# Turning the normalised tokens of groups 1 to 7 in 32x32 squares on VectorE, from pieces reloaded out of DRAM, in an attention and mixture-of-experts kernel

## The chip, the cores and the metric

One core of a Trainium2 chip runs the whole kernel. The metric is the device time of one execution in microseconds, as the median over several runs. A core has TensorE (matmul, with a separate weight load), VectorE, ScalarE, GpSimd, and SyncE (SP), which here only issues DMAs. Each engine runs its own instructions in order and waits for others on semaphores.

## What is computed

The input is 4 x 1024 tokens of 512 features. Each token is layer-normalised; attention and experts read the result xn, and both are added to x.

```python
xn = (x - mean) / sqrt(var + eps)
q, k, v = silu(xn @ Wq), silu(xn @ Wk), silu(xn @ Wv)      # 16 heads of 32
o = lightning_attn(q, k, v, log_decay)                     # chunks of 128 tokens, decaying state
o = group_rmsnorm(o * sigmoid(xn @ Wg1 @ Wg2)) * norm_w
y = x + o @ Wo
y = y + experts(xn)       # softmax(xn @ Wg), top 2 of 8; relu(xn @ w1) @ w2, capacity 1280
```

All of it is in float32. Products run as three passes of parts: each operand is split into a high part (rounded to the type that TensorE takes at full rate) and a low part (the rest), and high x high, high x low and low x high are summed.

## The kernel before

The 4096 tokens are 32 tiles of 128. Four tiles make a group (`g`, 0 to 7; `TPG` = 4, `SUPERS` = 8). Each group has 4 units (`i`, 0 to 3; `u = 4 g + i`), one for 4 heads. TensorE's loop over the units, in program order: `score`, `update_states` (a unit ahead where `updated_ahead` says so), `project_gate`, the k and the q projection of the next unit, `turn_kd`, `attend`. In unit 1 of a group the four output projections of the group before follow, and in unit 3 the small projection (gate and logits, `project_small`), `turn_logits`, and the four v projections of the next group.

For the projections the tokens must lie with features on partitions: xnT. A tile `xn[:, j, :]` (`j = t % 4`) is made by `normalise` on VectorE and stored to the DRAM tensor `xn_rows` by SP (`store_xn`), since the experts gather tokens from there. In unit 2 of a group TensorE turns the next group's four tiles with `turn_xn`: 4 transposes of 128x128 a tile, into four PSUM banks. ScalarE rounds them to `xnT_hi` (`xnT_high`), VectorE subtracts to `xnT_lo` (`xnT_low`); the k projection of the next group's first unit stands in unit 3. The second v projection of the next group waits for `g1_lo_made`, the low parts of the gate's inner product, made by VectorE (`gate_low`), behind ScalarE's `gate_high`, which is itself behind ScalarE's `oT_high` of unit 1.

VectorE's order in a unit: `states`, `mask` (4 instructions), `mean_square`, `scale_heads`, `turn_back` (of two units before), in unit 2 the four `xnT_low`, `gate_output`, `turn_gated`, `oT_low`. In unit 1 four `add_residual` follow, one for each output projection, with `norm_pair` between them and two `normalise` behind them; in unit 3 `choose`, `norm_pair` and two `normalise`. GpSimd multiplies kT and qT by their decays (`decayed_k`, `decayed_q`), raises small tensors to the power -1/2 (`head_scales`, `norm_scale`) and issues indirect DMAs for the routing.

SP's queue is one order written out by hand. At the start: four x tiles, Wq, Wk (eight pieces of 256 KB), the small weights, wg2, norm_w, four stores of xn, Wv and Wo. After that, in unit 1: four `store_y`, two `store_xn`, two `load_x`, then four `load_residual`. Each DMA stands behind its wait, and everything behind it waits too.

The weights `wq`, `wk`, `wv` are loaded as rows 128 t to 128 t + 127, since the k order of a projection is that of the turned tokens. The experts' weights are already loaded in another k order (rows q, t, d), because gathered tokens are turned in 32x32 squares by VectorE (`turn_gathered`).

## Time and profile before

| | us |
|---|---|
| median of 3 runs | 1984.32 |
| lowest, highest | 1983.89, 1984.41 |
| profiled execution | 1986.43 |
| its span on the core | 1984.7 |
| first group's start to its unit 0 | 0 to 32 |
| attention, units 0 to 31 | 32 to 532 |
| experts | 532 to the end |

The granted clock of TensorE is 1.0 in every stretch. All times in the rows below are microseconds from the span's start, in one profiled execution. A duration in a timeline overlaps with that of the next matmul, because they are pipelined; the pitch is the distance of two starts. "idle before" is how long the engine had nothing to do, with the instruction that released it.

### The profile page before, as it was taken

The numbers are of one execution on the slowest core, as the hardware profiler recorded it, in microseconds if no ns is written. First come the engines' busy times: TensorE is split into PE (matmuls) and PEld (weight loads), VectorE is DVE, ScalarE is ACT, GpSimd is POOL, SyncE is SP. The second block draws the span as 40 slices with busy tenths as digits, with TensorE's granted clock in tenths as the row PEclk, the third lists the DMA queues.
The fourth block names the chain that finished last, engine by engine and source line by source line (L and its number), as shares of the span: only waits on it lengthen the run. The fifth ranks groups of instructions, "written<-read, shape, count | busy, mean of one in ns | idle before, by whom it ended". The sixth has DMA issues, their size and how long they took to land.

```text
span 1984.7 us, 28995 instructions
## 1 busy us (share of the span) xinstructions
PE 1972.2 (99%) x11672; PEld 1631.0 (82%) x11672; DVE 906.7 (46%) x1839; ACT 552.5 (28%) x994; POOL 730.1 (37%) x608
## 2 busy tenths in 40 slices
PE   9999999999999999999999999999999999999998
PEld 7888888888888888888888888888888888888887
DVE  8777676777753234224323422432343234334311
ACT  6322232223332123124212312321242123123211
POOL 4645454545343324313342431333143324233321
PEclk9999999999999999999999999999999999999999
DMA  6112122211452134315233421522162125224121
GB/s 206 67 66 87 43 68 68 84 63 48 131 153 39 47 75 125 42 55 126 66 67 74 126 42 56 125 65 42 47 159 45 43 51 157 37 62 102 42 33 22
DMA packets 85638, 151.50 MB, mean 76 GB/s; under 512 B 18432, under 2 KB 18432, under 8 KB 85488
## 3 DMA queue, kind: packets, MB, share of 16 engines
q1 hardware_dynamic: 61312, 105.64, 16.8%
q0 software_dynamic: 24176, 43.76, 13.0%
q8 instruction: 106, 1.74, 0.4%
q14 instruction: 44, 0.36, 0.1%
HBM read 109.82 MB, written 39.53 MB: 75 GB/s over the span
## 4 chain that ended last, share of the span: by engine, by line
PE 97%; DVE 1%; SPq 1%; DMA 0%; issue 0%; POOL 0%; ACT 0%; DVEq 0%
PE bank L1383 47%; PE bank L1687 35%; PE bank L1519 5%; PE bank L1437 2%; PE bank L1508 2%; PE bank L1390 1%; PE bank L1502 1%; PE bank L1743 1%; PE bank L1730 1%; PE bank L1472 1%; PE bank L1411 1%; PE bank L1482 1%; DMA attn_raw<-in_L_attn_Wv 0%; PE bank L1531 0%; SPq L446 0%
## 5 line engine op out<-in xcount | busy, mean ns | idle before, releaser
L1303 DVE SCALAR_TENSOR_TENSOR h_lo<-bank,h_hi 128x512 fp32r<-128x512 f32 x254 | 175.3, 690 | 722.9 <-ACT h_hi L904 683.7
L682 POOL DMA_INDIRECT gathered<-xn_rows,gather_row x304 | 315.5, 1038 | 483.6 <-DVE x_blocks L1153 316.8
L1383 PE MATMUL bank<-xT_lo,w_hi 128*128 128x512 f32 x1024 | 398.5, 389 | 0.5 <-issue 0.5
L1383 PE MATMUL bank<-xT_hi,w_hi 128*128 128x512 f32 x1024 | 398.7, 389 | 0.0
L1383 PE MATMUL bank<-xT_hi,w_lo 128*128 128x512 f32 x1024 | 398.4, 389 | 0.0
L1687 PE MATMUL bank<-w_hi,h_hi 128*128 128x512 f32 x1016 | 395.2, 389 | 0.0
L1687 PE MATMUL bank<-w_lo,h_hi 128*128 128x512 f32 x1016 | 395.2, 389 | 0.0
L1687 PE MATMUL bank<-w_hi,h_lo 128*128 128x512 f32 x1016 | 395.2, 389 | 0.0
L904 ACT ACTIVATE h_hi<-bank 128x512 fp32r<-128x512 f32 x254 | 151.7, 597 | 795.5 <-PE bank L1383 756.3
L703 POOL DMA_INDIRECT out_rows<-y,add_row x64 | 103.9, 1624 | 435.7 <-ACT y L897 419.6
L1383 PEld LDWEIGHTS bank<-xT_lo,w_hi 128*128 128x128 f32 x1024 | 192.2, 188 | 40.9 <-issue 1.0
L1383 PEld LDWEIGHTS bank<-xT_hi,w_hi 128*128 128x128 f32 x1024 | 192.2, 188 | 40.8 <-issue 0.7
L1383 PEld LDWEIGHTS bank<-xT_hi,w_lo 128*128 128x128 f32 x1024 | 192.2, 188 | 39.9
L1687 PEld LDWEIGHTS bank<-w_lo,h_hi 128*128 128x128 f32 x1016 | 190.7, 188 | 39.8
L1687 PEld LDWEIGHTS bank<-w_hi,h_lo 128*128 128x128 f32 x1016 | 190.7, 188 | 39.6
L1687 PEld LDWEIGHTS bank<-w_hi,h_hi 128*128 128x128 f32 x1016 | 190.7, 188 | 39.4
L1123 DVE TENSOR_TENSOR w_lo<-raw_weights,w_hi 128x512 fp32r<-128x512 f32 x256 | 167.8, 684 | 84.8 <-ACT w_hi L802 64.9
L802 ACT CAST w_hi<-raw_weights 128x512 fp32r<-128x512 f32 x256 | 150.0, 618 | 98.3 <-DMA raw_weights<-in_L_ffn_w 78.8
L636 POOL TENSOR_TENSOR head_scale<-mean_sq,minus_half 128x16 f32<-128x16 f32 x32 | 104.4, 3264 | 20.7 <-DVE mean_sq L1025 20.2
L628 POOL DMA_INDIRECT slot_table<-record,slot_no x64 | 65.5, 1024 | 103.7 <-DVE slot_no L1069 47.4
L1018 DVE TENSOR_TENSOR scores<-bank,intra_decay 128x512 f32<-128x512 f32 x128 | 79.2, 681 | 0.4 <-PE bank L1437 0.3
L1163 DVE TENSOR_TENSOR xT_lo<-x_blocks,xT_hi 128x512 fp32r<-128x512 f32 x68 | 48.4, 711 | 52.3 <-ACT xT_hi L845 52.3
(225 smaller groups left out, 2298.5 us busy)
## 6 DMA issues: line engine op xcount, KB each, us to landing
raw_weights<-in_L_ffn_w SPq DMA_DIRECT2D x256, 256.0 KB
x_in<-in_L_attn_x SPq DMA_DIRECT2D x32, 256.0 KB, 4.0
xn_rows<-xn SPq DMA_DIRECT2D x32, 256.0 KB
x_res<-in_L_attn_x SPq DMA_DIRECT2D x32, 256.0 KB, 4.9
out_rows<-y_attn SPq DMA_DIRECT2D x28, 256.0 KB
gathered<-xn_rows,gather_row POOLq DMA_INDIRECT x304
out_rows<-y,add_row POOLq DMA_INDIRECT x88, 5.8
attn_raw<-in_L_attn_Wq SPq DMA_DIRECT2D x4, 256.0 KB, 4.7
```

The source lines that it names most:

```text
L628: pool.indirect_dma_start(table[:, :], bass.IndirectOffsetOnAxis(ap=slot_no[:, t, i:i + 1], axis=0), record[:, t, i, :], None, bounds_chec ...
L636: g_.tensor_tensor(head_scale[:, u % 2, :], mean_sq[:, u % 2, :], minus_half[:, :], ALU.pow).then_inc(S["head_scale_ready"], 1)
L682: pool.indirect_dma_start(xg[:, nth % 2, q * P:(q + 1) * P], None, xn_pieces, bass.IndirectOffsetOnAxis(ap=gather_row[:, col, q:q + 1], ax ...
L703: pool.indirect_dma_start(out[:, :], bass.IndirectOffsetOnAxis(ap=add_row[:, col:col + 1], axis=0), y[:, i, :], None, compute_op=ALU.add). ...
L802: a.copy(unit_parts(u)[0], raw[:, u % UNITS, :]).then_inc(S["ffn_hi"], 1)
L904: a.activation(h_parts(e, j, f)[0][:, 0:n * P], h_bank[f % 2][:, 0:n * P], ACT.Relu).then_inc(S["h_hi_ready"], 1)
L1018: v_.tensor_tensor(by_chunk(scores[:, r, :]), by_chunk(sc[r][:, :]), decay_cols(intra_decay[:, u % GROUPS * HPG + r, :]), ALU.mult).then_i ...
L1123: v_.tensor_tensor(lo, raw[:, u % UNITS, :], hi.bitcast(F32), ALU.subtract).then_inc(S["ffn_lo"], 1)
L1303: v_.scalar_tensor_tensor(lo[:, 0:n * P], h_bank[f % 2][:, 0:n * P], 0.0, hi[:, 0:n * P].bitcast(F32), ALU.max, ALU.subtract).then_inc(S[" ...
L1383: last = mm(dest, at(left[l], t), at_r(right[r], t), start=(i == 0), stop=(i == n - 1))
L1519: last = mm(bank[:, :], oT[l][:, t, part], (w_hi["o"], w_lo["o"])[r][:, t, :], start=(start and t == ks[0] and l == r == 0), stop=(stop an ...
L1687: last = mm(y_bank[i][:, :], hx[:, part], wx[c][:, f % FPC, :], start=(f == 0 and l == 0), stop=(f == FT - 1 and l == 2))
```

## The change

VectorE's transpose works on 32x32 squares: it turns each square in place, and doesn't move squares between partitions. So the tile must come with its feature quarters on the four partition quadrants. For groups 1 to 7 SP now reloads each tile from `xn_rows` after it was stored: four DMAs, one for each 32 tokens, put feature quarter q on quadrant q. VectorE turns the tile with one instruction, tile j into the space of tile j - 1 (tile 0 into a new buffer). The k order is then (q, t, d), and the weights of q, k, v, gate and router are loaded in the same order by `by_quad`. The first group is still turned by TensorE, but into the same order, with 16 small matmuls a tile (`turn_by_quads`).

```diff
+        def xn_blocks(j):
+            return xn_first_blocks[:, :] if j == 0 else xn[:, j - 1, :]
...
+        def by_quad(w):
+            return w.rearrange("(q t d) n -> t q d n", q=QUADS, t=DT)
...
+            def reload_pieces(t):
+                j = t % TPG
+                sp.wait_ge(xn_stored[j], 16 * (t // TPG + 1))
+                for i in range(QUADS):
+                    first = t * P + i * HD
+                    sp.dma_start(xn[:, j, i * P:(i + 1) * P], xn_dram[first:first + HD, :].rearrange("s (q f) -> q s f", q=QUADS)
+                                 ).then_inc(xn_pieces_loaded[j], 16)
...
-            sp.dma_start(small_raw[:, :, 0:HD], wg1.rearrange("(t p) n -> p t n", p=P)).then_inc(S["small_loaded"], 16)
-            sp.dma_start(small_raw[:, :, HD:], w_route.rearrange("(t p) n -> p t n", p=P)).then_inc(S["small_loaded"], 16)
+            for t in range(DT):
+                sp.dma_start(small_raw[:, t, 0:HD], by_quad(wg1)[t]).then_inc(S["small_loaded"], 16)
+                sp.dma_start(small_raw[:, t, HD:], by_quad(w_route)[t]).then_inc(S["small_loaded"], 16)
...
+            def turn_pieces(t):
+                j = t % TPG
+                dve.wait_ge(xn_pieces_loaded[j], 16 * QUADS * (t // TPG))
+                wait(dve, ("xn_turned", t))
+                v_.transpose(xn_blocks(j), xn[:, j, :]).then_inc(S["xn_turned"], 1)
...
+            def turn_by_quads(bank, rows_of_tile):
+                for t in range(DT):
+                    for q in range(QUADS):
+                        rows, first = slice(q * HD, (q + 1) * HD), q * P + t * HD
+                        last = mm(bank[rows, t * P:(t + 1) * P], rows_of_tile[:, first:first + HD], ident[:, :], start=True, stop=True)
+                return last
...
+            def project_next_k(g):
+                pe.wait_ge(S["xnT_hi_made"], TPG * (g + 1))
+                for nth, (w_part, x_part, t) in enumerate(hi_hi + lo_hi + hi_lo):
+                    if nth == 2 * DT:
+                        pe.wait_ge(S["xnT_lo_made"], TPG * (g + 1))
+                    last = mm(proj[1][:, :], w_part["k"][:, t, 0:P], x_part[:, t, :], start=(nth == 0), stop=(nth == 3 * DT - 1))
+                last.then_inc(S["k_projected"], 1)
...
-                if i == 2 and g < SUPERS - 1:
-                    pe.wait_ge(S["masked"], HPG * (u + 1))
-                    turn_xn(g + 1, lambda j: pe.wait_ge(S["k_ready" if j == 2 else "q_ready"], u + 2) if j > 1 else None)
```

The waits on `xnT_lo_made` in `score` and ahead of the gate projection of unit 3 are gone; the k projection in unit 3 (`project_next_k`) begins with the passes that need high parts only. On ScalarE `xnT_high` waits for the q projection as well, and `copy_kd` moves between its second and third tile.

TensorE at the hand-over from group 1 to group 2, unit 2 into unit 3 of group 1. Before:

```order
L1383 MATMUL bank<-xnT_lo,wq_hi 128x512
L1383 MATMUL bank<-xnT_hi,wq_lo 128x512
L1390 MATMUL bank<-ident,xn 128x128 x16
L1390 MATMUL bank<-ident,kdT 128x128 x3
L1502 MATMUL bank<-qdT,carry 128x128
L1502 MATMUL bank<-qdT,state 128x128 x3
L1508 MATMUL bank<-scores,v 32x128 x16
L1437 MATMUL bank<-qT,kT 128x128 x16
L1482 MATMUL bank<-v,kd 32x32 x12
L1472 MATMUL bank<-g1T_parts,wg_parts 128x512
L1383 MATMUL bank<-xnT_hi,wk_hi 128x512
```

And now:

```order
L1430 MATMUL bank<-xnT_hi,wq_lo 128x512
L1437 MATMUL bank<-ident,kdT 128x128 x3
L1554 MATMUL bank<-qdT,carry 128x128
L1554 MATMUL bank<-qdT,state 128x128 x3
L1560 MATMUL bank<-scores,v 32x128 x16
L1489 MATMUL bank<-qT,kT 128x128 x16
L1534 MATMUL bank<-v,kd 32x32 x12
L1524 MATMUL bank<-g1T_parts,wg_parts 128x512
L1613 MATMUL bank<-xnT_hi,wk_hi 128x512 x4
L1613 MATMUL bank<-xnT_hi,wk_lo 128x512 x4
L1613 MATMUL bank<-xnT_lo,wk_hi 128x512 x4
```

The 16 transposes of xn are gone, and the four passes with the low parts of the tokens stand last in the k projection.

VectorE in the same hand-over, from the end of unit 1 (`gated` is the gated attention output, `normed` the normalised one). Before:

```order
L1098 STREAM_TRANSPOSE turned_odd<-gated 128x512
L1118 TENSOR_TENSOR y_attn<-bank,x_res 128x512
L976 BN_STATS stats<-x_in 128x6 x2
L978 BN_AGGR moments<-stats 128x2
L979 BN_AGGR moments<-stats 128x2
L980 TENSOR_SCALAR var_eps<-moments 128x2
L1118 TENSOR_TENSOR y_attn<-bank,x_res 128x512 x3
L986 TENSOR_SCALAR xn<-x_in,moments,rstd 128x512 x2
...
L1108 STREAM_TRANSPOSE normed<-squares 128x512
L993 TENSOR_TENSOR xnT_lo<-bank,xnT_hi 128x4x128 x4
L1094 SCALAR_TENSOR_TENSOR gated<-tanh_g,bank 128x512
```

And now:

```order
L1140 STREAM_TRANSPOSE turned_odd<-gated 128x512
L1035 STREAM_TRANSPOSE xn_first_blocks<-xn 128x512
L1035 STREAM_TRANSPOSE xn<-xn 128x512
L1160 TENSOR_TENSOR y_attn<-bank,x_res 128x512
...
L1160 TENSOR_TENSOR y_attn<-bank,x_res 128x512
L1021 TENSOR_SCALAR xn<-x_in,moments,rstd 128x512 x2
L1160 TENSOR_TENSOR y_attn<-bank,x_res 128x512 x2
...
L1150 STREAM_TRANSPOSE normed<-squares 128x512
L1035 STREAM_TRANSPOSE xn<-xn 128x512 x2
L1027 TENSOR_TENSOR xnT_lo<-xn_first_blocks,xnT_hi 128x4x128
L1027 TENSOR_TENSOR xnT_lo<-xn,xnT_hi 128x4x128 x3
```

Two transposes stand ahead of the first residual and two ahead of the low parts; the two normalisations have moved ahead of the last two residuals; and the low parts read the turned tile from SBUF, where they read a PSUM bank.

SP's queue in unit 1 of the same group (`y_attn` is a finished tile of attention output). Before:

```order
L434 DMA out_rows<-y_attn 128x512 x4
L426 DMA xn_rows<-xn 128x512 x2
L422 DMA x_in<-in_L_attn_x 128x512 x2
L430 DMA x_res<-in_L_attn_x 128x512 x4
L426 DMA xn_rows<-xn 128x512 x2
```

And now:

```order
L454 DMA out_rows<-y_attn 128x512 x2
L437 DMA xn_rows<-xn 128x512 x2
L454 DMA out_rows<-y_attn 128x512
L445 DMA xn<-xn_rows 128x1x128 x8
L454 DMA out_rows<-y_attn 128x512
L433 DMA x_in<-in_L_attn_x 128x512 x2
L450 DMA x_res<-in_L_attn_x 128x512 x4
```

The two stores of xn have moved ahead of the last two of y, and eight reloads stand between, the last four of them for tile 3.

## Rows read from the trace of the kernel before

**Rows 1.** The page's part 4, shares of the chain that ended last, by engine.

```profile
PE 97%; DVE 1%; SPq 1%; DMA 0%; issue 0%; POOL 0%; ACT 0%; DVEq 0%
```

**Rows 2.** TensorE's waits, whole span: us in total, times, longest us.

```profile
PE bank L1508 <- DVE scores L1018: 1.0, 1, 1.0
```

**Rows 3.** The chain in order of time, group 1: start us, us, what.

```profile
103.78 0.33 PE bank L1390 x3
...
106.20 11.11 PE bank L1519 x48
...
124.31 2.07 PE bank L1390 x19
```

**Rows 4.** Timeline of TensorE, group 1: start us, us, engine, line, instruction.

```profile
124.15 1.91 PE L1390 MATMUL bank<-ident,xn 128*128 128x128 f32 x16
...
129.99 0.40 PE L1383 MATMUL bank<-xnT_hi,wk_hi 128*128 128x512 f32 x1
...
142.95 0.39 PE L1383 MATMUL bank<-wv_hi,xnT_hi 128*128 128x512 f32 x1
```

**Rows 5.** Timeline of ScalarE, units 2 and 3 of group 1.

```profile
124.84 2.05 ACT L757 CAST xnT_hi<-bank 128x512 fp32r<-128x512 f32 x4
...
138.57 0.62 ACT L808 CAST oT_hi<-normed 128x512 fp32r<-128x512 f32 x1
```

**Rows 6.** Timeline of VectorE, units 1 to 3 of group 1.

```profile
109.19 0.69 DVE L1118 TENSOR_TENSOR y_attn<-bank,x_res 128x512 f32<-128x512 f32 x1 [1.68 <-PE bank L1519]
...
117.96 0.99 DVE L986 TENSOR_SCALAR xn<-x_in,moments,rstd 128x512 f32<-128x512 f32 x2
...
123.60 0.17 DVE L1025 TENSOR_SCALAR mean_sq<-sum_sq 128x16 f32<-128x16 f32 x1
...
125.46 2.48 DVE L993 TENSOR_TENSOR xnT_lo<-bank,xnT_hi 128x512 fp32r<-128x512 f32 x4 [0.35 <-ACT xnT_hi L757]
128.36 0.69 DVE L1094 SCALAR_TENSOR_TENSOR gated<-tanh_g,bank 128x512 f32<-128x512 f32 x1 [0.42 <-PE bank L1508]
...
135.82 0.71 DVE L1108 STREAM_TRANSPOSE normed<-squares 128x512 f32<-128x512 f32 x1
139.23 0.69 DVE L1112 TENSOR_TENSOR oT_lo<-normed,oT_hi 128x512 fp32r<-128x512 f32 x1 [2.70 <-ACT oT_hi L808]
...
140.98 0.69 DVE L1012 CAST g1T_parts<-bank 32x512 fp32r<-32x512 f32 x1
```

**Rows 7.** Timeline of GpSimd, units 2 and 3 of group 1.

```profile
123.85 3.31 POOL L636 TENSOR_TENSOR head_scale<-mean_sq,minus_half 128x16 f32<-128x16 f32 x1 [0.52 <-DVE mean_sq L1025]
128.50 1.28 POOL L589 TENSOR_TENSOR qdT<-qT,q_decay 128x512 f32<-128x512 f32 x1 [1.33 <-PE bank L1508]
...
133.61 1.29 POOL L582 TENSOR_TENSOR kdT<-kT,k_decay 128x512 f32<-128x512 f32 x1 [1.05 <-ACT kT L777]
```

**Rows 8.** Timelines of GpSimd, then VectorE, unit 0 of group 0.

```profile
37.86 1.29 POOL L582 TENSOR_TENSOR kdT<-kT,k_decay 128x512 f32<-128x512 f32 x1
...
37.89 1.43 DVE L1083 SCALAR_TENSOR_TENSOR state<-state,chunk_decay,update 128x128 f32<-128x128 f32 x1
39.35 0.35 DVE L1084 SCALAR_TENSOR_TENSOR carry<-state,chunk_decay,update 128x128 f32<-128x128 f32 x1
```

**Rows 9.** SP's timeline; then DMA issues: KB each, median us to landing.

```profile
6.94 0.47 SPq L453 DMA_DIRECT2D small_raw<-in_L_attn_Wg  x1
...
x_in<-in_L_attn_x SPq DMA_DIRECT2D x32, 256.0 KB, 4.0
...
small_raw<-in_L_attn_Wg SPq DMA_DIRECT2D x1, 64.0 KB, 5.9
```

**Rows 10.** Timeline of TensorE: first group's start, and gathered tiles at 519.

```profile
9.06 2.02 PE L1390 MATMUL bank<-ident,xn 128*128 128x128 f32 x16
...
12.24 1.16 PE L1550 MATMUL bank<-xnT_hi,wq_hi 128*128 128x512 f32 x4 [0.29 <-ACT xnT_hi L757]
...
518.85 2.83 PE L1531 MATMUL bank<-ident,y 128*32 128x128 f32 x96
```

More of the change, by code:

```diff
@@ L255, in build @@
         x_res_loaded = [sem(f"x_res_loaded{i}") for i in range(TPG)]
+        xn_pieces_loaded = [sem(f"xn_pieces_loaded{i}") for i in range(TPG)]
         xn_stored = [sem(f"xn_stored{i}") for i in range(TPG)]
@@ L474, in _ @@
                         store_xn(t)
+                    for t in range(TPG, 2 * TPG):
+                        reload_pieces(t)
                     for t in range(2 * TPG, 3 * TPG):
@@ L487, in _ @@
                 if i == 1 and g > 0:
-                    for j in range(TPG):
-                        store_y(TPG * (g - 1) + j)
+                    store_y(TPG * (g - 1))
+                    store_y(TPG * (g - 1) + 1)
                     if g < SUPERS - 1:
@@ L755, in xnT_high @@
                 act.wait_ge(S["xn_turned"], t + 1)
-                wait(act, ("k_projected", GROUPS * (t // TPG)))
-                a.copy(xnT_hi[:, :, j * P:(j + 1) * P], turned_xn(t)).then_inc(S["xnT_hi_made"], 1)
+                wait(act, ("k_projected", GROUPS * (t // TPG)), ("q_projected", GROUPS * (t // TPG)))
+                a.copy(token_cols(xnT_hi, j), turned_xn(t)).then_inc(S["xnT_hi_made"], 1)
             def weights_high(n, ts=range(DT)):
@@ L864, in _ @@
                     for j in range(TPG):
+                        if j == 2:
+                            copy_kd(u + 1)
                         xnT_high(TPG * (g + 1) + j)
-                if i == GROUPS - 1 and g < SUPERS - 1:
-                    copy_logits(g + 1)
-                if u < ATTN_UNITS - 1:
+                elif u < ATTN_UNITS - 1:
+                    if i == GROUPS - 1:
+                        copy_logits(g + 1)
                     copy_kd(u + 1)
@@ L1242, in _ @@
                     oT_low(u - 2)
+                if i == 1 and g < SUPERS - 1:
+                    turn_pieces(TPG * (g + 1))
+                    turn_pieces(TPG * (g + 1) + 1)
                 if i == 1 and g > 0:
@@ L1527, in turn_first @@
                 pe.wait_ge(S["masked"], HPG * (ATTN_UNITS - 1) + sc.index(first_bank[i]) + 1)
-                for t in range(DT):
-                    for q in range(QUADS):
-                        rows, first = slice(q * HD, (q + 1) * HD), q * P + t * HD
-                        last = mm(first_bank[i][rows, t * P:(t + 1) * P], y[:, i, first:first + HD], ident[:, :], start=True, stop=True)
-                last.then_inc(S["x_turned"], 1)
+                turn_by_quads(first_bank[i], y[:, i, :]).then_inc(S["x_turned"], 1)
             pe.wait_ge(S["consts_made"], 6)
@@ L1540, in _ @@
             keep_clock(40)
-            turn_xn(0)
+            turn_first_xn()
             keep_clock(8)
```

56 lines of the change are left out of this document (34 added, 22 removed).

## The prediction

> **What bounds the kernel now.** I read the chain of work that ended last first: 97% of the span lies on TensorE, and VectorE, ScalarE, GpSimd and the queues together have a few per cent [rows 1]. Then TensorE's own waits: once it is set up, the longest is 1.0 us, once, for masked scores [rows 2]. So the kernel is a single line of TensorE work, and an instruction taken from it gives back its whole pitch, as long as the engine that takes over its job is not late. The question is therefore asked at the places where TensorE will newly have to wait. The stretch that matters is the hand-over from one group of 512 tokens to the next, seven times in the first 450 us; the experts behind it are not touched.
>
> **1. The transposes that go.** In group 1 the chain shows 3 transposes of kdT in 0.33 us, and 19 transposes (16 of xn and 3 of kdT) in 2.07 us [rows 3]. The 16 of xn therefore cost 2.07 - 0.33 = 1.74 us, 0.109 each. (Their duration in the timeline, 1.91 us together, overlaps with what follows [rows 4].) Seven hand-overs lose them: 7 x 1.74 = 12.2 us. TensorE has nothing to put in their place, since the order shows 112 of them gone and no new matmul in the loop.
>
> **2. The first group.** It keeps its transposes on TensorE but turns by quads: 64 small matmuls of 32 weight columns in place of 16. The same form in before, three tiles for the experts, took 2.83 us [rows 10], so 0.94 a tile against 2.02 / 4 = 0.50. The first tile can start at 9.06; the last ends at 12.8 in place of 11.1, and the first projection, which already waited 0.29 for the high parts of the last tile [rows 10], starts about 1.4 later. Besides this, SP issues the small weights in 8 DMAs in place of 2: 6 x 0.47 = 2.8 us [rows 9] by which wg2, norm_w, the stores of xn and Wv are issued later. What the landing does with it is not clear: small_raw took 5.9 us from issue to landing against 4.0 for an x tile four times its size [rows 9], so these DMAs wait in a line for the 3 MB ahead of them, and a later issue shortens that wait. The two delays run side by side, not one after the other. Whether there is slack is seen at the end of this start: TensorE waited 1.0 us for the scores of unit 0 [rows 2], so VectorE's chain is the late one there and hands every delay on. Bounds 1.4 (the turning alone) and 2.8 (the issue alone); I take **1.8**, nearer the first, since the queue looked full.
>
> **3. The pieces come back in time, by little.** VectorE normalises tiles 2 and 3 of the next group after the second out-projection now. Four out-projections take 11.11, 2.78 each [rows 3], the first residual starts at 109.19 [rows 6], so the second ends near 112.6 and the two tiles are written at 113.1 and 113.6. A store has no landing time in the trace; an x tile of the same size takes 4.0 [rows 9], so tile 2 is stored at 117.2, 4 reloads take 4 x 0.47 = 1.9 on SP, 4 more end at 121.0, and the last lands 4.0 later at 125.0. VectorE reaches its two transposes near 124.8 (its mean of squares ends at 123.77 [rows 6], two 0.7 us operations follow, all up to 0.9 us earlier since the two normalisations of 117.96 [rows 6] have moved ahead). Nothing is lost, or 0.2. Queued behind SP's wait for the store: the fourth y store, two x tiles and four residual tiles, none needed for 40 us. A page speaks against such a round trip: the Trainium skill, "DMA: Bandwidth & Descriptors", section "Anatomy of one DMA", gives each DMA about 2 us of fixed cost, most of it the receipt, longest when DRAM is written. Worked out from its figures (an estimate) the store would take 2.6 and the last reload 2.2, earlier than my 4.0 each; by that the term would be nothing.
>
> **4. High parts.** ScalarE starts them at 124.84 as before and does four in 2.05 [rows 5]; copy_kd now stands between (0.4), so they end near 127.4. TensorE comes to them 1.74 earlier than before: 129.99 - 1.75 = 128.24 [rows 4]. 0.8 us of slack. It needs the low parts only after eight matmuls, at 130.0, since the order of its passes has changed.
>
> **5. VectorE's added work and its lock.** Two transposes of 0.71 [rows 6] stand in unit 1 ahead of the first residual, where VectorE was idle for 1.68 us [rows 6]: nothing. Two more (1.3 by their pitch) stand in unit 2 ahead of the low parts. VectorE's line from there runs without a rest to 136.53 (start 135.82 plus 0.71 [rows 6]); it then waited 2.70 us for ScalarE's oT_hi, which itself waits for TensorE [rows 5, 6]. New end of that line: 136.53 + 1.3 - 0.9 (normalisations gone) - 0.77 (its waits of 0.35 and 0.42 around 125.46, for things that now come earlier) = 136.2. TensorE's side allows oT_hi from 138.57 - 1.75 = 136.8. By this alone nothing is late.
>
> But xnT_low now reads both operands from SBUF; so far one came from PSUM. The trace shows what such an instruction meets: a state update of two SBUF operands, otherwise 0.35 us, took 1.43 while GpSimd's kdT product ran from 37.86 for 1.29 [rows 8]. GpSimd's product qdT waits for the attention and started at 128.50; its pow from 123.85 ended at 127.16, now up to 0.9 earlier [rows 7]. So qdT now starts at 128.50 - 1.75 = 126.75, into the third and fourth low part: about 1.2 late. That pushes the state updates behind the start of the next kdT, 133.61 - 1.75 = 131.86 [rows 7], and they lose 1.3 more. With both, VectorE's line ends at 138.7, oT_hi starts there, and g1T_parts is complete 3.1 later as before (138.57 to 141.67 [rows 5, 6]), at 141.8. TensorE wants it for the second v projection at 142.95 - 1.75 = 141.2 [rows 4]: **0.6 late**. With one block or none it is in time. If the two small waits don't go, 1.35. Bounds 0 and 1.35 for each of six hand-overs; I take 0.6, since the arithmetic puts both products on top of VectorE: 6 x 0.6 = 3.6. The first hand-over is worse: unit 1 of group 0 has no out-projection, so no gap for its two transposes, and no normalisation is taken off. That is 2.2 more on VectorE's line, half of which I let pass through: 1.7 (0.2 to 2.6).
>
> The page's rule: the Trainium skill, "SBUF — State Buffer", section "Who interferes with whom", says that a VectorE instruction with two SBUF inputs and a GpSimd one that reads SBUF exclude each other for the whole instruction, whichever came first. The trace agrees in the row of 1.43. It doesn't say who wins when VectorE's next instruction is already queued; if VectorE, this term is nothing.
>
> **Sum**: -12.2 + 1.8 + 3.6 + 1.7 = -5.1 us. The profiled span was 1984.7, so 1979.6; the median of the runs is 1984.3, hence **1979.2**.
>
> **The rivals.**
> *A clean gain.* VectorE keeps the lock through its four low parts, or GpSimd's products fall between; then the hand-overs cost 0.2 in all and the start 1.4: -10.6, **1973.7**. For it: VectorE's rest of 2.70 us and the 1.2 us (142.95 - 141.7) that TensorE had in hand. Against it: both products move earlier by just what TensorE gains.
> *VectorE eats the gain.* Both blocks in each hand-over and the small waits stay: 6 x 1.35 = 8.1, first one 2.6, start 2.0: +0.5, **1984.8**. For it: VectorE has 2 x 1.3 us more per group, and whatever it is late by, TensorE gets no faster.
> *The round trip is late, and it gets slower.* If a store and a reload each take 5.9 us, as small_raw did [rows 9], and all 8 issues lie between: stored 119.1, issued 122.9, landed 128.8, and the high part of tile 3 is ready 1.4 later, 130.2 against 128.24: 2.0 per hand-over, 7 x 2.0 + 1.8 + 3.6 - 12.2 = +7.2, **1991.5**. It decides from a landing after about 127.8, 1.5 per hand-over. Against it: SP's queue is empty at 113, with 3 MB ahead of it only at the start.
> That the change would not do what it says has no case: the order has the transposes gone.
>
> **How the numbers follow.** Forecast 0.42, with its own range of 1976 to 1981.5; clean gain 0.26; gain eaten 0.25; slower 0.07. The range 1973.5 to 1986.0 takes in the first three and leaves out most of the last and a little on the fast side. What a measurement of this kernel can tell from no change is 0.2%, 4.0 us: faster means under 1980.3. The clean gain and some four fifths of the forecast lie there, 0.60; the rest of the forecast and the eaten gain make 0.33 for the same; slower 0.07.
>
> **What would show it.** The chain should have 16 transposes fewer in each hand-over, 1.74 us between the q projection and kdT's transposes gone. Step 2: the first projection at about 13.6, unit 0's attention at about 44. Step 3: no wait of the transposes on the reloads. Step 5: one or two of the low parts, and a state update, drawn out to about 1.3 us with a GpSimd product beside them, and TensorE idle before the second v projection on g1T_parts. If TensorE waits for xnT_hi in place of that, step 3 or 4 is wrong; if it waits for nothing, step 5.

## The result, and the profile after

The changed kernel takes 2017.9 us (median of 6 runs, 2016.0 to 2019.3) where the kernel before takes 1984.2 on the same chip (6 runs, 1983.5 to 1984.8). The ratio is 1.017, with a 95% interval of 1.0157 to 1.0184: 1.7% slower. Forecast were 1979.2, a range of 1973.5 to 1986.0, and a chance of 0.07 for slower. The profiled execution spans 2015.6 us, 30.9 more than before.

TensorE's waits are the first view to compare with [rows 2], where 1.0 us for scores was the longest once the engine was set up. Columns as there: engine, place, what it waited for, us in total, times, longest.

```profile
PE bank L1430 <- DVE wv_lo L1046: 10.4, 4, 4.8
PE bank L1598 <- ACT xnT_hi L789: 6.3, 1, 6.3
PE bank L1430 <- DVE g1T_parts L1054: 4.2, 7, 0.9
PE bank L1598 <- ACT wk_hi L799: 4.1, 2, 2.2
PE bank L1586 <- POOL ident L578: 2.7, 1, 2.7
PE bank L1430 <- issue: 2.3, 1, 2.3
PE bank L1613 <- DVE xnT_lo L1027: 0.7, 1, 0.7
PE bank L1560 <- DVE scores L1060: 0.3, 1, 0.3
```

Three rows wait for weights or for what stands behind them (wv_lo, wk_hi, and xnT_hi, whose copies stand behind Wq's on ScalarE). All of their seven waits lie in the first 53 us. The row of g1T_parts is the wait that the prediction's step 5 named; it comes once in each hand-over. The 2.3 for "issue" comes up below.

ScalarE's timeline at the start shows what the weights wait for (start us, us, line, instruction, and in brackets the idle time ahead of it with its releaser):

```profile
9.56 0.63 ACT L799 ACTIVATE wq_hi<-attn_raw 128x512 fp32r<-128x512 f32 x1 [2.42 <-DMA attn_raw<-in_L_attn_Wq]
12.23 0.63 ACT L799 ACTIVATE wq_hi<-attn_raw 128x512 fp32r<-128x512 f32 x1 [2.04 <-DMA attn_raw<-in_L_attn_Wq]
14.89 0.63 ACT L799 ACTIVATE wq_hi<-attn_raw 128x512 fp32r<-128x512 f32 x1 [2.03 <-DMA attn_raw<-in_L_attn_Wq]
17.58 0.63 ACT L799 ACTIVATE wq_hi<-attn_raw 128x512 fp32r<-128x512 f32 x1 [2.06 <-DMA attn_raw<-in_L_attn_Wq]
18.12 2.03 ACT L789 CAST xnT_hi<-bank 128x512 fp32r<-128x512 f32 x4
```

One piece of 256 KB arrives every 2.67 us; in before, four copies of wq_hi began and ended within 2.67 us. Now the same stretch by windows, first after, then before (stretch and its length; PE, PEld, DVE, ACT and POOL busy; granted clock, DMA share of 16 engines, GB/s):

```profile
12.00:15.00 3.00, 2.04 (x48) 1.60 (x36) 0.00 (x0) 0.74 (x2) 0.13 (x1) 1.00 0.26 98
...
12.00:34.00 22.00, 11.62 (x69) 8.23 (x58) 5.56 (x9) 6.35 (x11) 0.13 (x1) 0.70 0.30 97
```

```profile
4.00:10.00 6.00, 6.00 (x45) 5.89 (x43) 5.43 (x17) 4.90 (x13) 2.69 (x7) 1.00 1.05 396
```

After moves 98 GB/s with a share of 0.26, before 396 with 1.05: four engines' worth of work against sixteen, at the same rate for each busy engine (98 / 0.26 and 396 / 1.05 are both 377). The load of a weight tile now reads four strips of 32 rows, with the strip as its outermost dimension, of size 4. The Trainium skill, "DMA: Bandwidth & Descriptors", section "Why a DMA increments its semaphore by 16 and not by 1", says that the number of engines is the largest one up to 16 that divides the sizes of the slowest dimension on both sides; by that, 4. The trace agrees: a share of 0.26 is close to 4 of 16, 0.25.

The granted clock is the second thing in that stretch: 0.70 over 12 to 34 us, and 0.50 over 45 to 55, where 0.50 is the lower of the two levels (1.2 in place of 2.4 GHz). TensorE had idled 6.25 us, 1.95, 2.17 and 4.76 before it. In before the clock was 1.00 in both stretches.

SyncE's queue, which issues the loads (start us, us taken by the issues):

```profile
3.13 2.44 SPq L467 DMA_DIRECT2D attn_raw<-in_L_attn_Wq  x4
5.61 11.02 SPq L467 DMA_DIRECT2D attn_raw<-in_L_attn_Wk  x4
16.67 2.55 SPq L475 DMA_DIRECT2D small_raw<-in_L_attn_Wg  x1
...
34.18 3.29 SPq L467 DMA_DIRECT2D attn_raw<-in_L_attn_Wv  x4
```

Issuing Wk took 11.02 us; in before it took 1.87. So the queue doesn't only deliver late, it also takes new work late, and Wv, issued at 12.84 before, goes out at 34.18.

With the start of each unit's score products as milestones (from TensorE's timelines, us) the whole span can be laid side by side. "Hand-over" is the unit that ends a group, unit 3 to 4, 7 to 8 and so on; the transposes stood in the unit before it.

| stretch | before | after | difference |
|---|---|---|---|
| start to the first score | 32.29 | 65.57 | +33.3 |
| unit 0 | 10.87 | 9.54 | -1.3 |
| units 2, 6, ... 26 | 11.29, 10.98, 10.87, ... | 9.55, 9.24, 9.13, ... | 7 x -1.74 = -12.2 |
| first hand-over | 22.85 | 25.93 | +3.1 |
| six others | 22.84 to 23.11 | 23.79 to 24.40 | +6.9 |
| unit 29 | 23.13 | 20.86 | -2.3 |
| from unit 31 to the end of the span | 1469.2 | 1472.6 | +3.4 |

That makes 30.9. The expected gain is in the table to the hundredth, 1.74 for each of seven groups. Ahead of it stand 33 us at the start, for which the prediction has 1.8.

The row of unit 29 is not the change's, since kernels of the changed kind have the 2.3 us too. TensorE has two short stops for "issue" there (0.34 and 0.46 us in before) in the profiles of before and of experiments 1 to 8, which take 23.1 to 23.3 us for the unit, and none in those of the changed kernel and of experiments 9 to 12, which take 20.9. The profiled execution of before took 1986.4 us, 1.6 more than the slowest of its six other runs. So the two profiles lie 30.9 us apart where the medians lie 33.7 apart.

### The profile page after: what moved, and what is told of

Read it like the earlier page. It is cut to its first block, busy times and chain, and to the rows that moved or that the text cites. A ratio compares the mean times of both kernels' runs of the same rounds, so it can differ in the third digit from the quotient of the medians.

```text
span 2015.6 us, 29141 instructions
## 1 busy us (share of the span) xinstructions
PE 1977.5 (98%) x11672; PEld 1624.9 (81%) x11672; DVE 939.2 (47%) x1867; ACT 554.9 (28%) x994; POOL 736.2 (37%) x608
## 4 chain that ended last, share of the span: by engine, by line
PE 88%; DVE 6%; SPq 2%; issue 2%; DMA 1%; ACT 1%; POOL 0%; DVEq 0%
PE bank L1430 43%; PE bank L1743 35%; PE bank L1571 4%; DVE scores L1060 1%; PE bank L1799 1%; PE bank L1786 1%; PE bank L1489 1%; PE bank L1560 1%; DVE xnT_lo L1027 1%; DMA attn_raw<-in_L_attn_Wv 1%; PE bank L1554 1%; SPq L467 1%; PE bank L1437 1%; DMA xn<-xn_rows 1%; DVE xn L1035 0%
## 5 line engine op out<-in xcount | busy, mean ns | idle before, releaser
L1743 PEld LDWEIGHTS bank<-w_hi,h_lo 128*128 128x128 f32 x1016 | 190.7, 188 | 39.6
```

The lines of the kernel that those rows point to most:

```text
L1743: last = mm(y_bank[i][:, :], hx[:, part], wx[c][:, f % FPC, :], start=(f == 0 and l == 0), stop=(f == FT - 1 and l == 2))
```

## The experiments

Twelve kernels in three sets, each set on one chip with its own runs of before. The medians of before were 1987.3, 1986.8 and 1984.6; the differences below are to these. My theory was that the loads' pattern is the slow start; the rivals were the order in SyncE's queue, the turning by quads with the clock, and at the hand-overs VectorE held up by GpSimd (the lock of step 5) against the order of its copies and ScalarE's.

### 1. Plain weight loads in the changed kernel

```
-                rows = w[u % DT * P:(u % DT + 1) * P, :] if u // DT == WSET.index("o") else by_quad(w)[u % DT]
-                sp.dma_start(attn_raw[:, u % UNITS, :], rows).then_inc(attn_raw_loaded[u % UNITS], 16)
+                sp.dma_start(attn_raw[:, u % UNITS, :], w[u % DT * P:(u % DT + 1) * P, :]).then_inc(attn_raw_loaded[u % UNITS], 16)
```

> The changed kernel with one edit: the twelve loads of Wq, Wk and Wv take plain blocks of 128 rows again (the sums over features then pair wrong rows, so the attention's values are wrong; the work is the same; Wg1 and the router keep their order, so the routing is unchanged). Theory 1, the loads' pattern: each 256 KB load in four strips of 32 rows kept only a quarter of the DMA engines busy (98 to 105 GB/s and a share of 0.26 where before showed about 400 GB/s), and TensorE was 33 us late at the first score; the loads take about 0.65 us again, the first score comes within 3 us of the 32.3 us of before, and the time is 1979 to 1984 us, faster than before by up to 5. Theory 2, the queue's order (six more small loads and sixteen reloads on SyncE's queue): the start stays more than 15 us late, time over 2000. Theory 3, turning by quads on TensorE and the lower clock behind it: the start stays late, time over 2000.

Measured: 1992.4 us, 5.0 above before (ratio 1.003, 1.0018 to 1.0041) where the change cost 33.7. I had expected a time below that of before. The first score is at 37.8: 27.8 of the 33.3 us are back. Of what is left, SyncE's timeline shows the part of the small loads: one of the eight issues takes 2.19 us, and Wv goes out at 18.00 in place of 12.84, TensorE waiting 2.0 for it:

```profile
9.67 2.19 SPq L474 DMA_DIRECT2D small_raw<-in_L_attn_Wg  x1
...
18.00 2.63 SPq L466 DMA_DIRECT2D attn_raw<-in_L_attn_Wv  x4
```

So the pattern is the bulk, and the queue's order is real too: a part of the second theory. The hand-overs take as long as in the changed kernel (25.91 us the first, 23.80 to 24.40 the others); experiments 4 to 6 take that up.

### 2. The pattern alone, in the kernel before

```
-                sp.dma_start(attn_raw[:, u % UNITS, :], w[u % DT * P:(u % DT + 1) * P, :]).then_inc(attn_raw_loaded[u % UNITS], 16)
+                rows = w[u % DT * P:(u % DT + 1) * P, :] if u // DT == WSET.index("o") else w.rearrange("(q t d) n -> t q d n", q=QUADS, t=DT)[u % DT]
+                sp.dma_start(attn_raw[:, u % UNITS, :], rows).then_inc(attn_raw_loaded[u % UNITS], 16)
```

> The kernel before with one edit: its twelve loads of Wq, Wk and Wv take four strips of 32 rows each (the attention's values are then wrong, the work is the same). Theory 1, the pattern alone: 30 to 34 us slower than before, 2014 to 2018 us, with weight loads of about 2.66 us each at about 100 GB/s and a granted clock below 1.0 in the first 100 us. Theories 2 and 3 (the queue's order, the first group's turning): 1984 to 1986 us.

Measured: 2014.7 us, 27.4 above before (1.0137, 1.012 to 1.0154), the first score at 62.1, a clock of 0.56 over 12 to 34 us. That is less than the 30 to 34 expected; the eight small loads and the turning by quads aren't there, and the first score comes 3.5 us ahead of the changed kernel's. With nothing else of the change in it, the pattern alone costs 27 us.

### 3. The same order of features from another pattern

```
+                q, first = u % DT, u // DT * DT % UNITS
+                sp.dma_start(attn_raw[q * HD:(q + 1) * HD, first:first + DT, :],
+                             w[q * P:(q + 1) * P, :].rearrange("(t d) n -> d t n", t=DT)).then_inc(attn_raw_loaded[u % UNITS], 16)
```

> The changed kernel, whole and with the same order of features in Wq, Wk and Wv, but each of the same twelve loads of 256 KB brings another share: the 32 partitions of one quad for all four tiles of a matrix, with 32 rows as its outer dimension, where the changed kernel's load brings all 128 partitions of one tile with four strips as its outer dimension. A matrix is then whole only with its fourth load. Theory 1 in the form 'as many DMA engines as the outer dimension gives': the engines' share is near 1.0, a load takes 0.7 us, the start is 1 to 3 us behind that of plain blocks, time 1980 to 1987 us. Theory 1 in another form, 'rows that don't lie in one block in memory are slow' or 'few partitions are slow': loads stay at 100 to 200 GB/s, time over 1995. Theories 2 and 3: time over 2000.

Measured: 2000.9 us, 13.5 above before (1.007, 1.0054 to 1.0087). Neither form of theory 1 alone: the share is full, the rate is not. Its window:

```profile
12.00:15.00 3.00, 2.49 (x64) 2.05 (x52) 0.69 (x1) 2.63 (x6) 0.13 (x1) 1.00 1.08 209
```

All 16 engines are busy (1.08) and move 209 GB/s, half of before's 396 at 1.05. With an outer dimension of 32 the engines are all at work again, as they should be by the rule of the Trainium skill cited above. Something else in this form then halves what each engine moves. Rows are of 2 KB in all three forms; what differs from the plain block is that a load fills 32 partitions and not 128, and that each partition takes four rows that lie 32 rows apart in DRAM. Which of these it is I didn't separate.

### 4. Natural order everywhere

The order of features is turned round: the normalising instruction writes permuted columns, and after the 32x32 turning each tile of 128 partitions holds 128 features in a row. All weights, the experts' first ones too, load as plain blocks, the small ones in two DMAs.

```
-                v_.tensor_scalar(xn[:, j, :], x_in[:, j, :], moments[:, j, 0:1], rstd[:, j:j + 1],
+                v_.tensor_scalar(xn[:, j, :].rearrange("p (q t d) -> p t q d", q=QUADS, t=DT),
+                                 x_in[:, j, :].rearrange("p (t q d) -> p t q d", q=QUADS, t=DT), moments[:, j, 0:1], rstd[:, j:j + 1],
...
-                return w1[e].rearrange("(q t d) f -> t q d f", q=QUADS, t=DT)[i, :, :, c * D:(c + 1) * D]
+                return w1[e, i * P:(i + 1) * P, c * D:(c + 1) * D]
```

> The changed kernel, whole, with the order of features turned round: the normalising instruction writes its 512 columns permuted (feature t*128+q*32+d into column q*128+t*32+d), so that after the 32x32 turning each tile of 128 partitions holds features in their natural order; Wq, Wk, Wv, Wg1, the router's weights and the experts' first weights are all loaded in plain blocks of rows, the small ones in two loads again. Theory 1: start as plain blocks and 2 us less of small loads, 1977 to 1982 us; if the permuted writing makes the normalising instruction slower, 0.1 to 0.3 us more in four of them before the first projection. Theories 2: gains 3 us over the kernel with plain blocks for Wq, Wk, Wv alone. Theory 3: time over 2000. That the experts' first weights come faster should change nothing (their loads lie ahead of their use): 0 to 1 us.

Measured: 1987.6 us, that of before (1.0001, 0.9991 to 1.0011). That is 4.8 below experiment 1, 3.7 of it by the first score, so the small loads were worth a little more than the 3 expected (the other differences are the permuted writing and the experts' first weights, now plain too). The permuted writing costs nothing: the instruction takes 542 ns in both forms. The first score is at 34.10, 1.81 later than before: the turning by quads, 3.70 us against 2.02, and little else.

But I expected 1977 to 1982. With the start mended, the whole gain of 12.2 is still gone. The milestones say where: the hand-overs took 9.5 more than before, 3.05 the first and 0.7 or 1.5 in turn the others, the start 1.8, and the experts 1.1. The next two experiments take the hand-overs.

### 5. GpSimd's products made small

```
-                n = carried_chunks(u)
+                n = 1 if u % GROUPS == 0 and u > 0 else carried_chunks(u)
...
+                n = 1 if u % GROUPS == GROUPS - 1 and u < ATTN_UNITS - 1 else TPG
+                g_.tensor_tensor(by_chunk(qdT[:, :])[:, 0:n, :], by_chunk(qT[:, :])[:, 0:n, :],
+                                 q_decay[:, u % GROUPS, :].unsqueeze(1).to_broadcast([P, n, P]), ALU.mult).then_inc(S["qd_ready"], 1)
```

> The kernel with natural order (all weights in plain blocks, columns permuted by the normalising instruction; its time was that of before) with GpSimd's products qdT of units 3, 7, ... 27 and kdT of units 4, 8, ... 28 cut to their first chunk of 128 columns; the other chunks keep old values, so the attention's values are wrong. In the natural-order kernel the hand-overs of the groups took 9.7 us more than before (3.1 the first, 0.7 and 1.5 in turn the others) against 12.2 saved, and TensorE waited 0.33 and 0.90 for g1T_parts. Theory A, VectorE and GpSimd keep each other out: xnT_lo x3 falls from 2.98 to 2.0, the state step next to kdT from 1.19 to 0.35, the waits for g1T_parts from 4.2 us in total to under 1.5, and the time is 3 to 5 us below before. Theory B, VectorE simply has more work there, or the chain through ScalarE (oT_hi ahead of g1T_parts) is the cause, and GpSimd's products are not: the waits stay at 3.5 to 4.2 and the time within 1 us of before.

Measured: 1980.3 us, 6.5 below before (0.9965, 0.9952 to 0.9977), more than the 3 to 5 of theory A. Groups of VectorE's instructions between 60 and 520 us, natural order first, then with small products (count, busy us, mean ns):

```profile
L1026 DVE TENSOR_TENSOR xnT_lo<-xn,xnT_hi 128x512 fp32r<-128x512 f32 x21 | 20.8, 1045 | 0.0
...
L1026 DVE TENSOR_TENSOR xnT_lo<-xn_first_blocks,xnT_hi 128x512 fp32r<-128x512 f32 x7 | 4.5, 650 | 0.0
```

```profile
L1027 DVE TENSOR_TENSOR xnT_lo<-xn,xnT_hi 128x512 fp32r<-128x512 f32 x21 | 15.3, 780 | 0.0
```

The first low part of each group runs ahead of GpSimd's product and takes 650 ns. The other three averaged 1045 ns beside the product and 780 beside its small form. Over the whole natural-order kernel their median is 681 ns and the longest takes 1780: not all three are slow, but one is held up, by about the length of a product. (They don't fall to 681 in the mean, since a quarter of the product is left.) At the hand-over of group 2 the state step fell from 1.19 to 0.35:

```profile
199.07 1.19 DVE L1123 SCALAR_TENSOR_TENSOR state<-update,chunk_decay 128x128 f32<-128x128 f32 x1
```

```profile
195.61 0.35 DVE L1124 SCALAR_TENSOR_TENSOR state<-update,chunk_decay 128x128 f32<-128x128 f32 x1
```

The waits for g1T_parts fell from 4.2 us in total to 0.4, and the six later hand-overs took before's time within 0.05 us each; the first kept 1.4 of its 3.05. GpSimd's two products are shown as the cause of their lateness. That they exclude VectorE, and don't only slow it, rests on the one long instruction in three.

### 6. The gate's copies first

```
+                if i == GROUPS - 1 and g < SUPERS - 1:
+                    gate_high(g + 1)
                 if 1 < u < ATTN_UNITS - 1:
                     oT_high(u - 2)
...
-                    gate_high(g + 1)
```

(and in the same way gate_low ahead of oT_low on VectorE.)

> The natural-order kernel, whole, with one order changed in the units that end a group: ScalarE's two copies of g1T_parts stand ahead of its oT_hi, and VectorE's two ahead of its oT_lo. In the trace ScalarE stood idle 1.94 us for 'normed' with the g1T copies queued behind, and VectorE 0.69 and 0.37 us for ScalarE. Theory B (the chain through ScalarE): the waits for g1T_parts vanish, each hand-over is shorter by 0.65 or 1.2 us, 6 us in all, time 5 to 6.5 us below before. Theory A (VectorE is late by the lock, whatever the order): the copies by VectorE start only 1.4 us earlier, which is still enough for the waits of 0.33 and 0.90, so the same gain; the two differ in the trace: by A the xnT_lo and the state step stay at 2.98 and 1.19. Theory C, the wait only moves to what is queued behind (oT_lo, gated, v's bank): gain under 2 us.

Measured: 1981.4 us, 5.5 below before (0.997, 0.9959 to 0.9982), with all of the work in it. xnT_lo x3 still takes 2.98 and the state step 1.19, and no wait for g1T_parts is left. The lock delays VectorE as much as ever, but what stands last behind the delay is now oT_lo, for which TensorE doesn't wait. So both theories hold: the lock made VectorE late, and the order turned that into a wait. The hand-overs take 3.4 us more than before in place of 9.5, 1.9 of it the first. In the natural-order kernel ScalarE's line shows the turning point, copies of g1T_parts that were possible since 202.8 behind an oT_hi that wasn't:

```profile
205.78 0.62 ACT L838 CAST oT_hi<-normed 128x512 fp32r<-128x512 f32 x1 [1.94 <-DVE normed L1149]
206.31 0.57 ACT L819 CAST g1T_parts<-bank 32x512 fp32r<-32x512 f32 x1
```

### 7. The clock

```
-            keep_clock(8)
+            keep_clock(60)
...
+                    if n == "k" and w_part is w_hi and x_part is xnT_hi:
+                        keep_clock(14)
```

(and 30 and 12 in the same way in the v projection.)

> The changed kernel, whole, with dummy transposes of 0.11 us put where TensorE waits for weights: 52 more behind the first group's turning, 14 behind each of the four first passes of k, 30 ahead of the first v projection and 12 ahead of each of its next tiles. They keep the engine busy in waits of 6.3, 2.0, 2.2, 4.8, 2.1, 2.3 and 1.2 us. Theory 1 with a part for the clock: the granted clock, 0.70 in 12 to 34 us and 0.86 in 34 to 98, rises, the matmuls of the first v projections go at 0.23 instead of 0.43 us each, and the time is 6 to 12 us below that of the changed kernel (2006 to 2012 on a chip where before takes 1984), the rest being loads. Theory 1 without it: within 2 us of the changed kernel, since the loads alone set the pace.

Measured: 1.0167 times before (1.015 to 1.0184), the changed kernel's own ratio. The clock did what was wanted, 1.00 in all stretches:

```profile
12.00:34.00 22.00, 20.44 (x198) 18.04 (x190) 5.57 (x9) 6.47 (x12) 0.13 (x1) 1.00 0.31 98
```

The loads still come at 98 GB/s, the first score is at 64.3 in place of 65.6, and unit 0 then takes 10.88 in place of 9.54, since VectorE's chain (scores) sets its end. My 6 to 12 us were wrong: at this start slow matmuls cost 1.3 us at most, since TensorE waits for the next weight tile anyway, and unit 0 took that back.

That the whole time is the changed kernel's is luck. By the start of unit 4 this kernel is 2.2 us behind the changed one, with waits of 0.77 for scores and 1.29 for xnT_hi that I didn't follow, and it has the 2.3 of unit 29; in return it hasn't the stop of 2.3 us in the experts, and these take 1435.3 us from their first product to the last of its kind in place of 1438.5.

### 8 and 11. The stop of 2.3 us in the experts

Seven kernels of the changed kind (the changed one, experiments 1, 3, 4, 5 and 6, and later 9) had one stop of TensorE at the same instruction, 455 us behind the experts' first product, for 2.1 to 2.5 us. Here is that of the natural-order kernel, and what its DMA queues moved in 986 to 987 us (queue: packets, MB, share):

```profile
985.62 0.39 PE L1429 MATMUL bank<-xT_lo,w_hi 128*128 128x512 f32 x1
988.48 0.50 PE L1429 MATMUL bank<-xT_hi,w_lo 128*128 128x512 f32 x1 [2.48 <-issue]
```

```profile
q8 instruction: 1, 0.02, 6.0%
```

Nothing releases it, and the one packet of that microsecond belongs to the instruction queue. In all seven profiles such a packet of 16 KB starts within 0.4 us of the stop's start. Two kernels shift TensorE's instructions by waits that are long true, 128 of them in experiment 8 (on the natural-order kernel), 40 in experiment 11 (on that of experiment 6):

```
+            for _ in range(128):
+                pe.wait_ge(S["consts_made"], 1)
```

> The natural-order kernel, whole, with 128 more instructions at the very start of TensorE's program, waits on something long true, ahead of its wait for ident (there it stood idle 2.7 us). All four kernels of the changed kind so far show one stop of TensorE of 2.1 to 2.5 us that waits for nothing, 455.2 to 455.6 us behind the first matmul of the experts, before shows none there but 0.54 at 1187. Theory P (a place in TensorE's stream of instructions): the stop moves elsewhere or goes, and the time falls by up to 2.5 us or stays. Theory Q (an event in the work of that moment, a transfer or another engine): it stays at 455 us behind the first matmul of the experts with 2.1 to 2.5 us, and the time is that of before within 1 us.

> The gate-first kernel, whole, with 40 waits on something long true at the start of TensorE's program, ahead of the wait for ident. In the kernel with 128 of them (5.4 us later at the start, some 63 ns each) the stop of 2.3 us in the experts was gone and the experts took 1435.2 us from first to last first product, as before's 1435.0, against 1436.3 to 1438.5 in the others. Theory P (a place in the stream of instructions): 40 fit into the 2.7 us that TensorE waits for ident, so the start is unchanged within 0.3 us; if 40 places are enough the stop goes or changes size and the time is 1.5 to 2.5 us below the gate-first kernel, if not it stays at the same place. Theory Q (an event of the work): the stop stays whatever is put ahead.

Measured: with 128, 1990.6 us, 3.8 above before (1.0019, 1.0009 to 1.0028), and the start is the reason: TensorE's first wait is 8.1 us and not 2.7, and the first score comes at 39.6, 5.5 later; the stop is gone, and from the experts' first product to the last of its kind it is 1435.2 us, as in before (1435.0). With 40: 1976.5 us, **8.1 below before** (0.9963, 0.9948 to 0.9977), no stop, the first score 0.56 later. On the same chip the kernel of experiment 9, which has the stop, is 5.1 below. TensorE's busy time in 520 to 1000 us, with the 40, then without:

```profile
520.00:1000.00 480.00, 479.93 (x2122) 396.39 (x2121) 182.02 (x349) 126.98 (x227) 157.32 (x135) 1.00 0.34 82
```

```profile
520.00:1000.00 480.00, 477.67 (x2139) 394.38 (x2139) 182.99 (x352) 127.31 (x227) 158.07 (x135) 1.00 0.34 82
```

Of theories P and Q, P is borne out: with the same number of instructions ahead the stop came at the same instruction in seven profiles of seven, and with 40, 128 or the 174 matmuls of experiment 7 more ahead of it, it is gone, in one profile each. That fetching instructions is its cause fits the packets but is not shown: 65 such packets come from the experts' start to the end in the natural-order kernel (windows of the trace, 530 to 1985 us), and one of them falls into a stop. Why this one is open.

### 9. Reloads in another form

```
-                for i in range(QUADS):
-                    sp.dma_start(xn[:, j, i * P:(i + 1) * P], xn_dram[first:first + HD, :].rearrange("s (q f) -> q s f", q=QUADS)
-                                 ).then_inc(xn_pieces_loaded[j], 16)
+                for q in range(QUADS):
+                    sp.dma_start(xn[q * HD:(q + 1) * HD, j, :].rearrange("s (i f) -> s i f", i=QUADS),
+                                 xn_dram[t * P:(t + 1) * P, q * P:(q + 1) * P].rearrange("(i s) f -> s i f", i=QUADS)
+                                 ).then_inc(xn_pieces_loaded[j], 16)
```

> The gate-first kernel (natural order, copies of g1T_parts ahead of oT), whole, with the reloads cut another way: each of the four loads of a tile brings the 32 partitions of one quad with 32 rows as its outer dimension instead of all 128 partitions with four quads as its outer dimension. In the gate-first kernel the 16 reloads of the first group took SyncE 12.5 us and moved 75 to 90 GB/s at a share of 0.3; the weight loads of the quad-rows kernel ran at about 206 GB/s in this shape. Theory R, the reloads cost nothing anyway (VectorE waited 0.4 us for them in all): time within 1.5 us of the gate-first kernel, 5 to 6.5 us below before, though the sixteen reloads are through in under 9 us. Theory S, the slow reloads make the first hand-over late (1.9 us over before there, with a wait of 0.7 for xnT_lo and 0.8 for scores): the first hand-over shortens by 1 to 1.9 us and the time by as much.

Measured: 1979.5 us, 5.1 below before (0.9973, 0.9963 to 0.9982), as experiment 6 within the intervals. The sixteen reloads of the first hand-over (tokens of group 1) took 8.6 us of SyncE in place of 12.5, and that hand-over 24.75 in place of 24.74. Theory R: they cost nothing. What its profile has better, 2.3 us, lies in unit 29, 20.87 in place of 23.15. TensorE's program is the same in experiments 6 and 9, so this is not a matter of its place alone. All eight profiles of the first two sets have these 2.3 us, none of the four of the third, and the medians of before (1987.3, 1986.8, 1984.6) fall between the sets by as much: it seems to go with the chip or the time of the set and cancels in a ratio to before. Its cause stays open.

### 10. The first group in plain transposes

```
-                    turn_by_quads(first_xn_bank[j], xn[:, j, :]).then_inc(S["xn_turned"], 1)
+                    turn(first_xn_bank[j], xn[:, j, :], DT).then_inc(S["xn_turned"], 1)
```

(its rows are then stored by 16 DMAs in pieces of 32 columns.)

> The gate-first kernel, whole, with the first group's tokens kept in natural columns and turned by 16 plain 128x128 transposes as before; its rows are stored permuted by four DMAs a tile in pieces of 32 columns, behind all weight loads. Theory T, the turning by quads costs what the trace shows (3.7 against 2.0 us): the first score comes 1.5 to 2 us earlier, at 32.3 to 32.7 us, and the time is 1.5 to 2 us below the gate-first kernel (6.5 to 8 below before). Theory U, the weights are as late anyway: the first score gains under 0.5 us. If the 8192 small pieces of the stores hold up the loads or the normalising of group 1: 1 to 4 us lost at the first hand-over.

Measured: 1985.8 us, level with before (1.0004, 0.9994 to 1.0013), and 6.6 worse than the kernel without it (5.5 below before). The first score came at 32.46, 1.5 earlier, as theory T says. Then TensorE waited 7.2 us in unit 0, for a reason on the queue:

```profile
18.65 13.38 SPq L441 DMA_DIRECT2D xn_rows<-xn  x16
32.08 1.94 SPq L433 DMA_DIRECT2D x_in<-in_L_attn_x  x4
```

```profile
PE bank L1444 <- DVE carry L1133: 7.2, 1, 7.2
```

The stores hold SyncE for 13.4 us, the next group's tokens are issued at 32.1 in place of 19.3, VectorE waits 7.9 us for them, and its state steps stand behind that. The price was larger than the 1 to 4 I had allowed.

### 12. All three together

Experiments 9, 10 and 11 in one kernel, no other edit.

> The gate-first kernel, whole, with all three: reloads by quad rows, first group in plain transposes, 40 waits. If the three add up as their theories T, S and P say: 4 to 6 us below the gate-first kernel, 0.5 per cent below before; if only the first group's turning counts, 1.5 to 2 us below it.

Measured: 1986.9 us, 2.3 above before (1.0013, 1.0004 to 1.0023). The 7 us of experiment 10 are in it (7.6 here), and a stop of 2.71 us is back, at another place, 810 us, again with a packet of the instruction queue at its start. Experiment 10, whose TensorE program lacks only the 40 waits, has stops of 0.38 at 814 us and of 1.36 at 1718. Forty waits are no remedy, they happen to fit one program.

## Why the prediction was wrong, point by point

- **Step 1, right.** 1.74 us for each group, seven times.
- **Step 2, the step that failed.** It counts the turning by quads and six issues, and takes the twelve weight loads over as they were, though the change alters their pattern; no sentence prices it. "1.4 and 2.8" were no bounds. Experiments 1 and 2 put that term at 29 us (33.7 less 5.0) and 27. A row for it was at hand: the experts' first weights load in this very pattern in before, and from 459 to 464 us they come at about 98 GB/s with a share of 0.26. What step 2 did price was right for its first part, 1.5 to 1.8 for the turning (experiments 10, 4) against its 1.4, and wrong in "the two delays run side by side": the eight small loads cost 3.7 us on top at the first score (37.80 against 34.10, experiments 1 and 4), because each later issue stands ahead of Wv.
- **Step 3, right in its result, off in its sizes.** Stores land after 2.0 to 2.6 us and not 4.0; in group 1 a reload takes SyncE 0.51 to 0.81 and not 0.47, and the last one landed 5.5 behind its issue. There VectorE waited 0.24. Experiment 9 shows that faster reloads bring nothing. Of the two times that the step works out from figures of the Trainium skill, the store's 2.6 came out and the reload's 2.2 did not. The section that it cites, "Anatomy of one DMA", is on DMAs that GpSimd issues, and SyncE issues these.
- **Step 4, right.** No hand-over of the changed kernel waits for xnT_hi.
- **Step 5, right in its mechanism, too small in its size.** Low parts and a state step drawn out beside GpSimd's products, g1T_parts late at the second v projection: as forecast, and experiment 5 shows the cause. These rows answer to [rows 6, 7]:

```profile
160.07 2.97 DVE L1027 TENSOR_TENSOR xnT_lo<-xn,xnT_hi 128x512 fp32r<-128x512 f32 x3
...
165.84 1.26 DVE L1129 SCALAR_TENSOR_TENSOR state<-state,chunk_decay,update 128x128 f32<-128x128 f32 x1
```

```profile
160.09 1.80 POOL L621 TENSOR_TENSOR qdT<-qT,q_decay 128x512 f32<-128x512 f32 x1
...
165.62 1.34 POOL L614 TENSOR_TENSOR kdT<-kT,k_decay 128x512 f32<-128x512 f32 x1 [0.99 <-ACT kT L809]
```

  They also answer what step 5 left open, who wins with both queued: the three low parts stood in VectorE's queue in a row, and qdT, which asked at 160.09, was through by 161.89, so GpSimd got in behind the first of them (0.65 for that and 1.28 for its product are 1.9, about its 1.80). The waits for g1T_parts are 4.2 us, seven of my 0.6, but the hand-overs lengthened by 10.0 in all: those of the six later with a wait of 0.32 to 0.34 by 0.7 to 1.1, those with 0.71 to 0.85 by 1.4 to 1.6, and the first, where 0.7 for xnT_lo and 0.3 for scores come in, by 3.1. Why a wait costs about twice its length there I didn't follow. My 5.3 should have been 9.5 to 10.
- **The experts**, "not touched", were 3.4 us longer (1.1 in experiment 4), 2.3 by a stop that comes with the place of instructions in TensorE's program and no work of the change; the other 1.1 stays open.
- **Rivals.** The slower one had the wrong mechanism: the round trip was never late. *VectorE eats the gain* (1984.8) is about what the change would have given without step 2's hole: the natural-order kernel measured level with before, its hand-overs 9.5 us longer (10.7 in the rival) and its start 1.8 (2.0).

## What to carry to other kernels

When a change alters the order of data in memory, list every DMA whose pattern it touches and price each by the row of a transfer in the same pattern, with its share of the engines, not by its bytes; here 3 MB at a quarter of the engines outweighed seven groups of saved work. The permutation belongs where it is free, here in the output pattern of an instruction that runs anyway. And when an engine's lateness is shared by two consumers, let the one come first for whom the bounding engine waits: that took the loss at the hand-overs from 9.5 to 3.4 us without making anything faster.

## What the runs showed of the hardware that I had not expected

- A load with four strips of 32 rows as its outer dimension keeps a quarter of the DMA engines busy (share 0.26, 98 GB/s; the changed kernel and experiment 2). One that fills 32 partitions, with 32 as its outer dimension, keeps all busy (1.08) and moves 209 GB/s, against 396 for a plain block into 128 partitions (experiment 3; not separated further).
- A queue with slow transfers ahead makes issuing slow as well: 11.02 us for four issues that otherwise take 1.87.
- A low clock (0.70 of full speed over 12 to 34 us, 0.50 over 45 to 55) cost 1.3 us at most at this start, since TensorE was waiting anyway (experiment 7).
- A product of GpSimd gets in between VectorE's instructions that are already queued: of three low parts in a row one takes up to 1780 ns and the others 681.
- TensorE stopped for 2.1 to 2.5 us for "issue" at an instruction that was the same in seven profiles, and the stop was gone when 40 or 128 instructions were put ahead (experiments 11 and 8). One of 2.7 stood elsewhere in experiment 12. A packet of the instruction queue starts within 0.4 us of each of these eight stops. Programs of equal work differ by that much in time (experiments 9 and 11: 5.1 and 8.1 us below before).
